# A recurrent mixing layer on one core: the first norm's transpose moved one iteration ahead, and a new order of the steps

## The reference, cut to what matters

```python
xn = _ln(x, ln1_w, ln1_b)
sx = _token_shift(xn, state[:, i1])
xxx = jnp.tanh((xn + sx * maa_x) @ maa_w1).reshape(b, l, 5, 1, EXTRA_MAA)
xxx = jnp.matmul(xxx, maa_w2).reshape(b, l, 5, E)
x5 = xn[:, :, None] + sx[:, :, None] * (maa_stack + xxx)
w = jnp.exp(-jnp.exp(time_decay + jnp.tanh(x5[:, :, 1] @ decay_w1) @ decay_w2))
r = (x5[:, :, 3] @ Wr.T).reshape(b, l, H, S)
k = (x5[:, :, 0] @ Wk.T).reshape(b, l, H, S)
v = (x5[:, :, 2] @ Wv.T).reshape(b, l, H, S)
g = jax.nn.silu(x5[:, :, 4] @ Wg.T)
...
def step(s, rkvw):
    r_t, k_t, v_t, w_t = rkvw
    a = k_t[:, :, :, None] * v_t[:, :, None, :]
    out = jnp.einsum('bhk,bhkd->bhd', r_t, u * a + s)
    return (a + w_t[:, :, :, None] * s, out)
...
x = x + att * g @ Wo.T
xn2 = _ln(x, ln2_w, ln2_b)
sx2 = _token_shift(xn2, state[:, i0])
xk = xn2 + sx2 * ffn_maa_k
xr = xn2 + sx2 * ffn_maa_r
rr = jax.nn.sigmoid(xr @ ffn_Wr.T)
kk = jnp.square(jax.nn.relu(xk @ ffn_Wk.T))
x = x + rr * (kk @ ffn_Wv.T)
```

## Time and profile before

| | us |
|---|---|
| median of 3 runs | 795.35 |
| lowest and highest | 793.9, 798.16 |
| profiled execution, device time | 795.61 |
| its span from the first to the last instruction | 793.8 |
| PE busy in the span | 705.9 |
| DVE, POOL, ACT busy | 513.6, 376.7, 324.7 |

### The profile page before, as it was taken

The page is one execution under the profiler, slowest core; times in us unless marked ns, Lnnn a source line. Parts: engine busy times, 40 slices in busy tenths (PEclk is TensorE's granted clock), DMA queues, the critical chain, the costliest instruction groups (busy, mean ns, idle before and its releaser), DMA issues.

```text
span 793.8 us, 17668 instructions
## 1 busy us (share of the span) xinstructions
PE 705.9 (89%) x7412; PEld 491.4 (62%) x7412; DVE 513.6 (65%) x767; ACT 324.7 (41%) x639; POOL 376.7 (47%) x223
## 2 busy tenths in 40 slices
PE   5986899997999889998799979998799978998797
PEld 4763677465674667556664665746665556755673
DVE  5638865695567774597556966677736965479441
ACT  2231843247332753427532483326433375325311
POOL 1248426763458435573257634584255732674000
PEclk9997899999999989999999999999999999999799
DMA  7910001010020201010010200202010000100000
GB/s 205 377 28 27 9 2 48 6 62 3 1 54 1 61 3 35 21 53 9 2 50 5 61 2 1 53 2 62 2 41 14 28 8 2 53 2 28 2 1 26
DMA packets 19275, 28.79 MB, mean 36 GB/s; under 512 B 5888, under 2 KB 11776, under 8 KB 18176
## 3 DMA queue, kind: packets, MB, share of 16 engines
q1 hardware_dynamic: 19200, 27.67, 11.0%
HBM read 18.35 MB, written 4.19 MB: 28 GB/s over the span
## 4 chain that ended last, share of the span: by engine, by line
PE 51%; issue 15%; POOL 14%; DVE 11%; ACT 7%; DMA 0%; POOLq 0%; DVEq 0%; ACTq 0%
PE FB L563 17%; PE BAB L820 7%; POOL pp L488 7%; PE FA L838 5%; PE FB L571 5%; PE FA L872 2%; ACT half L1048 2%; PE BAB L797 2%; PE FA L639 2%; DVE kvs L1357 2%; PE BAB L555 2%; PE FA L859 2%; PE BAB L733 2%; POOL mixes L453 2%; POOL mixes L451 1%
## 5 line engine op out<-in xcount | busy, mean ns | idle before, releaser
L488 POOL TENSOR_TENSOR pp<-rT,kT 128x2048 f32<-128x2048 f32 (+1 forms) x32 | 108.6, 3406 | 51.7 <-DVE rT L1229 51.7
L451 POOL TENSOR_TENSOR mixes<-mixes 128x1024 f32<-128x1024 f32 x30 | 72.0, 2400 | 127.9 <-ACT mixes L971 127.9
L453 POOL TENSOR_TENSOR mixes<-mixes,xnT 128x1024 f32<-128x1024 f32 x30 | 71.8, 2392 | 2.4
L563 PE MATMUL FB<-mixes,wk_s 128*128 128x256 f32 x256 | 66.1, 417 | 5.8 <-POOL mixes L453 3.5
L1321 DVE TENSOR_REDUCE half<-half 128x256 f32<-128x2048 f32 (+2 forms) x32 | 64.4, 2014 | 0.6
L504 POOL TENSOR_TENSOR acc<-acc,half 128x512 f32<-128x512 f32 x32 | 41.1, 1283 | 49.5 <-DVE half L1321 48.3
L563 PE MATMUL FB<-mixes,wv_s 128*128 128x256 f32 x256 | 60.8, 382 | 2.5 <-issue 1.5
L563 PE MATMUL FB<-mixes,wg_s 128*128 128x256 f32 x256 | 62.1, 392 | 0.0
L563 PEld LDWEIGHTS FB<-mixes,wk_s 128*128 128x128 f32 x256 | 52.1, 208 | 15.9 <-POOL mixes L453 4.5
L971 ACT ACTIVATE mixes<-FA,cols_s 128x256 f32<-128x256 f32 x116 | 45.4, 481 | 38.4 <-PE FA L639 33.4
L838 PE MATMUL FA<-wide,fk_s 128*128 128x256 f32 x256 | 57.2, 381 | 3.5 <-DVE wide L1472 2.2
(11 more groups left out here) (160 smaller groups left out, 1336.7 us busy)
## 6 DMA issues: line engine op xcount, KB each, us to landing
pp<-x SPq DMA_DIRECT2D x8, 512.0 KB, 3.8
xt<-x SPq DMA_DIRECT2D x8, 512.0 KB, 3.8
vp<-vT SPq DMA_DIRECT2D x128, 32.0 KB, 1.9
out<-wide SPq DMA_DIRECT2D x7, 512.0 KB, 3.0
wv_s<-wv SPq DMA_DIRECT2D x1, 1024.0 KB, 5.1
wk_s<-wk SPq DMA_DIRECT2D x1, 1024.0 KB, 7.6
wr_s<-wr SPq DMA_DIRECT2D x1, 1024.0 KB, 8.7
wg_s<-wg SPq DMA_DIRECT2D x1, 1024.0 KB, 10.8
```

The source lines that it names most:

```text
L451: nc.gpsimd.tensor_tensor(slot, slot, sx, ALU.mult).then_inc(s_["mixm_ready"], 1)
L453: nc.gpsimd.tensor_tensor(slot, slot, xnT[:, :, 1:L + 1], ALU.add).then_inc(s_["mix_ready"], 1)
L488: ins = nc.gpsimd.tensor_tensor(pp[:, i % 2, 0:size].rearrange("p (n i j) -> p n i j", i=m, j=m), spread(r.unsqueeze(3), 3, m), spread(k.u ...
L563: ins = nc.tensor.matmul(dst[:, c * L:(c + 1) * L], weight[:, q, c * P:(c + 1) * P], src[:, q, :], start=(q == 0), stop=(q == C - 1))
```

## The change

The transpose of the first norm is no longer a front step. As `n_turn` it belongs to the stage `n_`, so one iteration earlier: PE transposes the normed `x` of the next sequence into `FA` behind the copy of the last second product of the present one, and ACT writes `xnT` once POOL has finished the last mix. The wait for the feed-forward products moves from there to `f_m20`, and the first feed-forward step waits until `xnT` is written.

`c_fk` is cut into four steps by input group, and each `c_fr` and `c_fv` into two halves, `b_wo` into four pieces. The products are the same. All four tables are written anew. In `main`, the first three quarters of `c_fk` now stand ahead of `b_score0`, the transpose stands near the end behind `f_r0`, and `f_k2` and `f_k3` stand among the four `b_apply` steps. Both second norm transposes, `b_apply3` and `b_wo` have new neighbours. On ACT, `f_lora0` stands ahead of the copies of `v`, `b_decays` ahead of `b_kv0`, and half of the copy of `r` ahead of the second norm. On DVE `f_xin` stands behind `b_mul1`, on POOL `f_sx` stands first.

```diff
-            b_apply1 b_apply2 b_apply3 f_k2 f_k3 f_v0 f_m23 b_gn0 f_v1 b_gn1 f_v2 b_wo0 f_m24 b_wo1 f_v3 f_r0
+            f_dec1 f_dec2 f_m22 b_acc f_k0 f_k1 b_apply0 f_k2 b_apply1 b_apply2 f_k3 b_apply3 f_m23 f_v0 f_v1
...
-            def f_norm(b, par, n):
+            def n_turn(b, par, n):
                 if first(b):
                     pe.wait_ge(c_loaded, 16 * 4)
                 pe.wait_ge(s_["xhat_ready"], b + 1)
                 if not first(b):
                     pe.wait_ge(s_["mixe_ready"], NMIX * b)
-                    pe.wait_ge(s_["mul_ready"], T * (b - 1))
                 transpose_channels(FA, xhat).then_inc(s_["xhatT_ready"], 1)
...
-                if not first(b):
+                elif isinstance(b, int) and b == 1:
                     pe.wait_ge(s_["xnT_ready"], b + 1)
+                else:
+                    pe.wait_ge(s_["mul_ready"], T * (b - 1))
...
-            def c_fk(b, par, n):
-                loaded("fk")
-                for q in range(C):
+            def c_fk(q):
+                def run(b, par, n):
+                    if q == 0:
+                        loaded("fk")
                     pe.wait_ge(s_["xk_ready"], C * b + q + 1)
                     if q == 0 and not last(b):
                         pe.wait_ge(s_["mixe_ready"], NMIX * (b + 2))
+                        if not (isinstance(b, int) and b == B - 2):
+                            pe.wait_ge(s_["xnT_ready"], b + 3)
...
+            def token_half(dst, weight, src, t, h):
+
+                for q in (2 * h, 2 * h + 1):
+                    ins = nc.tensor.matmul(dst[:, t * E:(t + 1) * E], src[:, q, t * P:(t + 1) * P], big[weight][:, q, :],
+                                           start=(q == 0), stop=(q == C - 1), skip_group_check=True)
+                return ins
```

More of the change, by code:

```diff
@@ L816, in run @@
                         loaded("wo")
-                    for q, t in (((0, 0), (0, 1), (1, 0), (1, 1), (2, 0), (3, 0)), ((2, 1), (3, 1)))[part]:
+                    for q, t in (((0, 0), (0, 1)), ((1, 0), (1, 1)), ((2, 0), (3, 0)), ((2, 1), (3, 1)))[part]:
                         if t == 0:
@@ L821, in run @@
                                                start=(q == 0), stop=(q == C - 1), skip_group_check=True)
-                    ins.then_inc(s_["wo_ready"], 1)
+                    if part >= 2:
+                        ins.then_inc(s_["wo_ready"], 1)
                 return run
@@ L879, in _ @@
             for t in range(T):
-                steps.update({f"b_kv{t}": b_kv(t), f"b_gn{t}": b_gn(t), f"b_wo{t}": b_wo(t),
-                              f"b_norm2{t}": b_norm2(t), f"c_fv{t}": c_fv(t),
-                              f"c_fr{t}": c_fr(t)})
+                steps.update({f"b_kv{t}": b_kv(t), f"b_gn{t}": b_gn(t),
+                              f"b_norm2{t}": b_norm2(t)})
+                for h in range(2):
+                    steps.update({f"c_fv{t}{h}": c_fv(t, h), f"c_fr{t}{h}": c_fr(t, h)})
+            steps.update({f"b_wo{part}": b_wo(part) for part in range(4)})
+            steps.update({f"c_fk{q}": c_fk(q) for q in range(C)})
             steps.update(f_m20=f_m20, f_pair1=f_pair(1), f_pair3=f_pair(3))
```

101 lines of the change are left out of this document (53 added, 48 removed).

## The result

| | before | changed |
|---|---|---|
| median, us | 795.72 | 805.53 |
| lowest and highest, us | 793.9, 798.16 | 800.96, 805.82 |
| profiled execution, us | 795.61 | 805.41 |
| its span, us | 793.8 | 803.6 |

The ratio is 1.0085, with a 95% interval from 1.0045 to 1.0125 (the quotient of the two medians, of four runs each, is 1.0123): the changed kernel is slower. The predicted 800.0 us is short of the median by 5.5 us. The measured time lies at the upper end of the whole range, 790 to 806, and outside the main case's own, 797.5 to 803. So the sign of the main case was right and its size was not: 4.65 us were forecast, and the medians are 9.8 apart.

The account below looks back on a forecast made before the run. PE, busy 705.9 of 793.8 us, was taken to bound the kernel. The loop's +4.25 us, +1.0 ahead of it and -0.7 in the last iteration made +4.55: 800.2 us, or 800.0 against the median; whole range 790 to 806.

Parts of the forecast that it names:

- main case: The forecast itself, whole kernel: a small loss, 797.5 to 803 us, chance 0.40.
- The loop: Six main iterations: 555.25 to 559.5 us, +4.25, from 5 x 0.92 transpose, 6 x 0.2 fetch, 2 x 1.35 clock.
- The applications and the root: Main iteration: last application ends at 476.0, not 474.1; POOL holds DVE's second root instruction, so scaling stays at 481.3.
- kv: Main iteration: kv matmuls start unchanged, about 41.5 us behind the feed-forward keys, with about 1.5 us of PE wait ahead.
- rival B: Main iteration: v copies start right behind the transposes, so kv comes 1.1 us earlier; 790.9 us, chance 0.20.
- The waits behind: Main iteration: PE waits 1.6 us ahead of the values, 1.9 more ahead of the output projection, which stays at 486.92.
- Fetch: Instruction-fetch stops inside the applications: about 0.5 us remain, 0.2 reaching the chain per iteration; bounds 0 and 1.2 us.
- Clock: Keys in main: two of six iterations fall to 1.2 GHz, costing 1.35 us each; bounds none and six.
- Rival D: Whole loop: the new waits drop PE to 1.2 GHz in every iteration; 805.4 us, up to 808, chance 0.15.
- Quarter steps: Added waits inside the keys cut into quarters: between 0 and 0.1 us, so nothing.
- The ends: Two iterations ahead of the loop: pauses absorb the later score chain, transpose lengthens the end; +1.0 us (0 to 2).
- ACT and POOL at nothing: Transpose's parts on ACT (xnT) and POOL (the difference): costed at nothing, both engines being idle there before.

Follow-up runs that it names:

- Experiment 10: Kernel with the gate between statistics and norm and f_xin behind b_mul4, plus ACT copying v before the small tanh and TensorE's old order there: 788.94 us, 0.9901.
- Experiment 9: Three kernels side by side: changed kernel again, 804.72 us; with DVE's gate between statistics and norm, 797.39; with f_xin also behind b_mul4 in second, 794.22.
- experiment 5: Kernel before, with two of the four key blocks among the applications on TensorE in main: 798.94 us, ratio 1.0007.
- The control: Changed kernel, unaltered, run once more: 804.72 us, ratio 1.0103.
- experiment 4: Changed kernel's code with all tables as before, apart from the transpose, which stands at the iteration's end: 804.92 us, ratio 1.0101.
- experiment 7: Kernel before, with key blocks among the applications and DVE's statistics and norm behind the gate in main: 809.29 us, ratio 1.0144.
- gate between: Changed kernel with DVE's gate between statistics and norm in second and main: 797.39 us, ratio 1.0007.
- experiment 6: Changed kernel with DVE's statistics and norm behind the gate in main: 801.51 us, ratio 1.0049.
- experiment 1: Changed kernel with f_xin back behind the last doubling product (b_mul4) on DVE in second: 801.27 us, ratio 1.0063.
- experiment 2: Changed kernel with f_m22 and the second decay projection (f_dec2) back ahead of the applications on TensorE in second: 803.46 us, ratio 1.0089.
- experiment 3: Changed kernel with the tables first and second as before on all engines, the transpose still at the iteration's end: 804.29 us, ratio 1.0094.

## Why the prediction was short

*The loop: right, with errors that cancel.* Forecast +4.25, measured +3.66 and +4.25 in two profiles. The transpose costs PE its 0.9 us at the end, unhidden, as worked out: the stretch from the projection to the next keys is 19.2 us where it was 18.35. The sixth iteration, without transpose, was put at 91.83 and takes 90.08: that is 1.75 too much. The undisturbed ones were put at 92.75 and take 93.2 to 93.5: some 0.6 too little, five times. The 1.2 us for fetch were not needed, and the clock took 0.8 less than forecast. That the sum came out is in part luck. (The prediction's 92.8 us for the four lengthened iterations of the kernel before is 92.9.)

*The applications and the root.* I kept the scaling at its old time, because POOL would hold the root's second instruction. The applications end 2.4 us later than before, not 1.9 (63.16 against 60.76 behind the keys). The root begins just when POOL is done, so nothing holds it and nothing is gained either: the scaling starts 68.4 us behind the keys, 67.9 before. That half microsecond passes to the output projection (74.0, forecast 73.5).

*kv.* Forecast 41.6, measured 41.6 to 41.9, with 1.42 us of wait ahead (1.5 forecast). The step was right, and rival B did not come true because the table has the tanh first. Experiment 10 shows that this is what decided: reversed, kv comes 1.1 us earlier.

*The waits behind.* Ahead of the values 1.6 was forecast and 1.32 measured. Ahead of the output projection it was 1.9, measured 1.6 to 1.8, ended by the gate, as said. What I did not draw from it is that the norm ahead of the gate, harmless before, had become a price of its own. The norm itself has less time than before, not more. In the kernel before it ends 46 us ahead of its transpose in the next iteration, and the projection waited 0.28 us for the gate behind it:

```profile
485.44 1.00 DVE L1140 TENSOR_SCALAR kvs<-pp,mv,rs 128x512 f32<-128x512 f32 x2 [1.26 <-POOL rs L425]
...
532.12 1.09 PE L555 MATMUL FA<-ident_s,kvs 128*128 128x128 f32 x8
```

In the changed kernel it ends 12 us ahead, but PE reaches the projection about 1 us earlier (72.2 us behind the keys, 73.3 before), and the gate comes half a microsecond later. Experiment 9 puts the place of the norm at 7.3 us.

*Fetch.* Stops of about 0.5 us were forecast, 0.2 of each on the chain. Inside the applications of the loop none over 0.5 is left; those of 0.42 to 0.44 ahead of the first application stood in the kernel before too. So the stops went, as said and by experiment 5 too, and the term should have been nothing.

*Clock.* Two of six key blocks at 1.2 GHz were assumed, two came (380.77 and 568.73; periods 94.59 and 94.09). The price was 1.1 and 0.8 us rather than 1.35. The control had three. Ahead of the loop no clock term was forecast, and one was there (below). Rival D did not come true: what its time resembles (805.4) was reached another way.

*Quarter steps.* 0 to 0.1 was forecast. No row shows a cost, but no run here takes them alone: experiment 4 has them side by side as before.

*The ends: the step that failed.* "The pauses there take it up" was said of the part ahead of the loop, +1.0 with a bound of 2. It measured +7.1. In that part the transpose costs 0.9, and the first projections ran 1.5 us slower in the profiled execution, which is no matter of the change: the kernel before's own part, run again inside experiments 5 and 7, gave 137.11 and 135.93. Against the mean of its three profiles, 136.0, the excess is 6 us; the mean of the four profiles of the changed order, 140.6, gives 4.6. Experiment 9 removes 4.2 us of these with the place of one step, and what is left in three profiles (136.89, 136.99 and 137.88) is 0.9 to 1.9 us, where the forecast had 1.0. I looked at `f_xin`'s new place only for what it does to PE, at the length that it had before, and took the order of DVE in that iteration for harmless because the loop has the same order with slack behind it. In the loop it also lasts 3.3 to 4.0 us, but kv waits for ACT there, and nothing is lost.

That 1.0 fits what is left is luck, as the parts show. The first column runs from the end of the first r projection to the start of the scan.

| us, one value for each profile | r to scan | scan to first application | first application to keys |
|---|---|---|---|
| order of before (its own profile, experiments 5 and 7) | 41.4, 42.2, 41.4 | 7.0, 7.0, 7.0 | 36.6, 36.5, 36.6 |
| changed order (its own, the control, gate between) | 43.0, 43.9, 42.7 | 6.2, 6.2, 6.2 | 40.5, 41.0, 40.5 |
| changed order in experiment 6 | 42.0 | 4.4 | 39.8 |
| `f_xin` behind (experiments 1, 9, 10) | 41.4, 41.4, 41.5 | 4.3, 4.3, 4.3 | 40.4, 40.5, 40.5 |

The first column has `f_xin`'s collision, the second the race. The third is longer by 3.2 to 4.4 us in every profile with the changed order, and only 0.9 of it is the transpose. Most of it lies between the first and the last application, where PE now has more products to do and does them at a lower granted clock (0.64, 0.94 before). These are the two stretches, before and changed:

```profile
98.30:103.74 5.44, 5.16 (x266) 4.45 (x265) 2.86 (x1) 4.40 (x10) 2.05 (x2) 0.94 0.02 6
101.40:110.43 9.03, 9.03 (x289) 7.08 (x289) 3.59 (x1) 5.41 (x11) 5.97 (x3) 0.64 0.02 4
```

So with `f_xin` put back, 2.7 us won at the race and some 3 us lost behind it nearly cancel, and the forecast had neither. No experiment takes that loss alone: experiment 2 shortens the third column to 39.0, and the second grows to 7.1.

*The last iteration.* -0.7 was forecast, -0.95 measured.

*ACT and POOL at nothing.* Right for the changed kernel's order. Not right for any order: the copy waits for POOL's last mix to let go of the tile, and in the old order this made the keys wait 2.34 us (experiment 3).

## What to carry to other kernels

When an instruction moves on DVE or POOL, price it by what the other of the two does at the new place, not by its old duration: the same four instructions took 1.7 and 4.3 us here. When a step is moved away and an engine arrives earlier at a later wait, look at what stands ahead of the step that ends that wait: a norm ahead of the gate cost next to nothing before the move and 1.6 to 1.8 us an iteration behind it. With the norm in its old place the move was a loss, with the gate between the statistics and the norm there was none, and with the order of before at two more places it was a gain. A prologue needs its own check, because slack that the loop has behind an order may not be there.

## What the runs showed of the hardware

In the pairs measured here DVE and POOL exclude one another by whole instructions, and which one waits is a matter of which starts first. The norm, one SBUF tensor and two columns, took 1.00 us free and 4.71 beside POOL's mix; `f_xin`, two SBUF tensors, 1.66 and 4.26. The states' spreading beside mix 1 took 5.8 us where DVE was first and 7.5 where POOL was. DVE's products out of PSUM were not touched (2.29 us beside POOL's product 3 at 69.61, the same as elsewhere). Where POOL is first (by 0.55 us in the changed kernel), the first application of the changed order comes 1.9 us later behind the scan than where DVE is first, and the same order of steps took 138 us to the same place in one execution and 141 to 142 in three.

```profile
69.61 2.29 DVE L1325 TENSOR_TENSOR half<-BAB,vp 128x2048 f32<-128x2048 f32 x1
```
